# A two-layer transformer on one core: a third add on GpSimd, four rows summed by TensorE, and a softmax moved to the next pass

## The reference

```python
# 1: attention of 16 heads of 8 channels, bias -slope[h] * |i - j|
probs = softmax(q @ k.T / sqrt(8) + bias);  x = ln(x + (probs @ v) @ W_out.T + b_out)
# 2: 8 experts (top 2) and a shared one; c is the gate's weight of an expert
y = sum_e c[:, e] * ((silu(x @ W1[e] + B1) * (x @ W3[e] + B3)) @ W2[e] + B2);  x = ln(x + y + z)
# 3: a token looks back at 44 fixed offsets, of which 16 different ones are below 256
scores = stack([(q * shift(k, off)).sum(-1) * scale for off in OFFSETS], -1) + pos_bias
attn = softmax(scores)
out = sum_i attn[..., i] * shift(v, OFFSETS[i])
x = ln(x + (out * sigmoid(x @ w_gate + b_gate)) @ w_out + b_out)
# 4: 8 linear experts, top 2
x = ln(x + sum_e w[:, e] * (x @ expert_w[e].T))
```

## Time and profile before

| | |
|---|---|
| median of 3 runs | 1566.03 us |
| the profiled execution | 1564.01 us |
| its span, first to last instruction | 1562.2 us |
| mean granted clock of TensorE in it | 0.975 |
| instructions | 35071 |

### The profile page before, as it was taken

The page is one execution under the profiler, slowest core; times in us unless marked ns, Lnnn a source line. Parts: engine busy times, 40 slices in busy tenths (PEclk is TensorE's granted clock), DMA queues, the critical chain, the costliest instruction groups (busy, mean ns, idle before and its releaser), DMA issues.

```text
span 1562.2 us, 35071 instructions
## 1 busy us (share of the span) xinstructions
PE 1472.7 (94%) x12384; PEld 1171.0 (75%) x12384; DVE 1239.5 (79%) x3646; ACT 933.9 (60%) x1868; POOL 685.3 (44%) x644
## 2 busy tenths in 40 slices
PE   4899999999999999999999999999999999998855
PEld 2677788778778787788788778878887788776633
DVE  4567788888888888888888888888888888776656
ACT  1666756666666566666766666666566676654411
POOL 0024455554434455543445554334455543455531
PEclk9999999999999999999999999999999999999867
DMA  4324443344444334444443344344334434433321
GB/s 145 127 86 136 134 128 108 113 134 109 113 136 126 125 101 129 140 103 115 129 135 106 112 139 122 99 136 126 119 107 130 139 100 116 126 92 82 83 51 46
DMA packets 83563, 179.75 MB, mean 115 GB/s; under 512 B 9771, under 2 KB 65835, under 8 KB 66219
## 3 DMA queue, kind: packets, MB, share of 16 engines
q1 hardware_dynamic: 83390, 177.52, 39.9%
HBM read 151.80 MB, written 25.43 MB: 113 GB/s over the span
## 4 chain that ended last, share of the span: by engine, by line
PE 82%; DVE 8%; DMA 3%; issue 3%; POOL 2%; SPq 1%; ACT 1%; DVEq 0%; POOLq 0%; ACTq 0%
PE bTU L572 8%; PE bPV L543 8%; PE bPV L521 8%; PE bTU L573 8%; PE bS L560 7%; PE bTU L490 7%; PE bTU L463 6%; PE bTU L505 6%; PE b L581 4%; PE bS L563 3%; PE bTU L507 3%; PE b L454 2%; DVE mneg L1027 2%; PE b L437 1%; POOL prod L1098 1%
## 5 line engine op out<-in xcount | busy, mean ns | idle before, releaser
L1027 DVE TENSOR_REDUCE mneg<-bS 128x2 bf16<-128x512 f32 x512 | 339.6, 687 | 64.9 <-PE bS L563 63.4
L1090 POOL TENSOR_TENSOR prod<-prod 128x1024 f32<-128x1024 f32 x64 | 150.6, 2353 | 473.1 <-DVE prod L939 473.1
L1098 POOL TENSOR_TENSOR prod<-kC,qC 128x512 f32<-128x512 f32 x256 | 307.8, 1243 | 13.6 <-issue 13.6
L721 ACT ACTIVATE P<-bTU 128x512 f32<-128x512 f32 x512 | 287.7, 596 | 31.3 <-PE bTU L507 24.8
L1110 POOL TENSOR_TENSOR h<-ub,gBcb 128x256 f32<-128x256 f32 x256 | 183.8, 730 | 276.0 <-DVE ub L1040 264.7
L560 PE MATMUL bS<-stack 96*128 96x256 bf16 x1024 | 225.5, 279 | 15.9 <-DVE mneg L1027 7.8
L731 ACT ACTIVATE sil<-bTU,b 128x256 f32<-128x256 f32 x288 | 136.6, 475 | 155.5 <-PE bTU L573 148.3
L505 PE MATMUL bTU<-stack 97*128 97x256 bf16 x1024 | 215.2, 275 | 1.4 <-DMA stack<-mT 0.5
L563 PE MATMUL bS<-dist,identh 128*128 128x128 f16 x1024 | 200.1, 222 | 0.0
L507 PE MATMUL bTU<-dist,identh 128*128 128x128 f16 x1024 | 193.5, 220 | 0.0
L572 PE MATMUL bTU<-x1T,w 128*128 128x256 f32 x576 | 178.7, 392 | 1.1 <-DVE ub L1040 1.0
(11 more groups left out here) (156 smaller groups left out, 2634.0 us busy)
## 6 DMA issues: line engine op xcount, KB each, us to landing
prod<-d_w SPq DMA_DIRECT2D x64, 1024.0 KB, 9.5
stack<-d_parts SPq DMA_DIRECT2D x192, 192.0 KB
gBcb<-d_cB SPq DMA_DIRECT2D x32, 1024.0 KB, 5.5
d_parts<-parts SPq DMA_DIRECT2D x96, 128.0 KB, 2.0
d_w<-wT SPq DMA_DIRECT2D x32, 256.0 KB, 2.1
xT<-in_xT SPq DMA_DIRECT2D x32, 128.0 KB, 2.3
x<-in_x SPq DMA_DIRECT2D x32, 128.0 KB, 2.2
out_x<-xout SPq DMA_DIRECT2D x32, 128.0 KB, 1.9
```

The costliest lines, as they stand in the source:

```text
L721: act_f(P[k % 8][:].rearrange("p a b -> p (a b)"), bTU[turn_bank("ST", k)][:], ACT.Exp, scale=SLOPES[head(k)]).then_inc(actA2.done("exp", ...
L1027: v.tensor_reduce(mneg[:, :, k], bS[k % 2][:].rearrange("p (a b) -> p a b", a=TT), op=ALU.max, axis=AX.X, negate=True).then_inc(dveS.done( ...
L1098: tt_(prod[e % 2][:, 2 * p:2 * p + 2, :], shifted(kC, p), qC[:].unsqueeze(1).to_broadcast([128, 2, T]), ALU.mult).then_inc(poolC1.done("pr ...
```

## The change

Four things change. C2.sm sums four rows instead of eight, since GpSimd now makes a third add (C2.add.2: rows 8 to 11 onto rows 0 to 3, once the first two are done). The softmax of block 3 (steps scT, mx, exp, sum, wT, dw, wb, now named Cs) runs one pass later, in the pass of C2. Because C1.vg still runs in the pass before, the values `vC`, the gate `tg` and the residual `x2b` get two buffers each, and the scores `scs` no longer share one with `wT`. And all five orders are new.

```diff
-LAG = {..., "B2": 4, "C1": 4, "C2": 5, "C2n": 6,
+LAG = {..., "B2": 4, "C1": 4, "Cs": 5, "C2": 5, "C2n": 6,
     "pe": """
-        A1.qk S.s.0 S.s.1 B2.z A2.ST.0 S.s.2 S.s.3 A2.ST.1 A1.v A2.ST.2 A2.ST.3 S.s.4 A2.ST.4 S.s.5 A2.ST.5 A2.ST.6
+        B2.z A1.qk A1.v A2.ST.0 A2.ST.1 S.s.0 Cs.scT A2.ST.2 S.s.1 A2.ST.3 A2.ST.4 S.s.2 A2.PV.0 B.xT A2.ST.5
...
     "act": """
-        A1.qk  A2.exp.0 A2.exp.1 A2.exp.2 A2.exp.3 A2.exp.4 A2.exp.5 A2.exp.6 A3n.nm C2n.nm A2.exp.7 B.xT
+        A1.qk A2.exp.0 A2.exp.1 A2.exp.2 A2.exp.3 A3n.nm C2n.nm B2.nm Cs.exp B.xT A2.exp.4 D.xT C1.xT A2.exp.5
...
     "pool": """
-        C2.add.0 C2.add.1 C1.prod.0 C1.prod.1 C1.prod.2 C1.prod.3 C1.prod.4 C1.prod.5 C1.prod.6 C1.prod.7 A3.xbo
-        C2.xb B.h.1 B.h.2 B.h.3 B.h.4 B.h.5 B.h.6 B.h.7 B.h.8""",
+        C1.prod.0 C1.prod.1 C1.prod.2 C1.prod.3 C1.prod.4 C1.prod.5 C1.prod.6 C2.add.0 C1.prod.7 B.h.1 B.h.2 B.h.3
+        B.h.4 C2.add.1 B.h.5 C2.add.2 A3.xbo C2.xb B.h.6 B.h.7 B.h.8""",
...
-        for p in range(2):
-            pe.wait_ge(poolC2.sem, poolC2.count(e, "add", p))
-            for x in range(4):
-                i = mm(o[:, 0:T], ident[:], pv[e % 2][:, 8 * p + x, :], start=(p == 0 and x == 0),
-                       stop=(p == 1 and x == 3))
+        pe.wait_ge(poolSum.sem, poolSum.count(e, "add", 2))
+        for x in range(4):
+            i = mm(o[:, 0:T], ident[:], pv[e % 2][:, x, :], start=(x == 0), stop=(x == 3))
...
-        pool.wait_ge(dveC2.sem, dveC2.count(e, "pv", 4 * n + 3))
-        tt_(pv[e % 2][:, 8 * n:8 * n + 4, :], pv[e % 2][:, 8 * n:8 * n + 4, :], pv[e % 2][:, 8 * n + 4:8 * n + 8, :],
-            ALU.add).then_inc(poolC2.done("add", n), 1)
+        if n < 2:
+            pool.wait_ge(dveC2.sem, dveC2.count(e, "pv", 4 * n + 3))
+        else:
+            pool.wait_ge(poolSum.sem, poolSum.count(e, "add", n - 1))
+        to, frm, rows_ = ((0, 4, 4), (8, 12, 4), (0, 8, 4))[n]
+        tt_(pv[e % 2][:, to:to + rows_, :], pv[e % 2][:, to:to + rows_, :], pv[e % 2][:, frm:frm + rows_, :],
+            ALU.add).then_inc(poolSum.done("add", n), 1)
```

More of the change, by code:

```diff
@@ L61 @@
+        B.ab.8 C1.sc M.mT""",
     "dve": """
[L62 to L66, removed]
+        B2.res D2.mom N.root.0 A1.rest A1.v N.root.1 S.max.0 N.root.2 N.root.3 Cs.mx S.max.1 S.max.2 Cs.sum S.max.3
@@ L70 @@
+        B.h.4 C2.add.1 B.h.5 C2.add.2 A3.xbo C2.xb B.h.6 B.h.7 B.h.8""",
     "sp": """
-        C2.wb A1.part.0 D2.out A1.part.1 A1.part.2 X.xT B.cT A3.x A1.rows.0 B.cb A1.rows.1 A1.rows.2 C1.dw M.m C1.wb""",
+        Cs.dw A1.part.0 A1.part.1 Cs.wb B.cT C2.wb B.cb X.xT A1.part.2 A1.rows.0 A3.x A1.rows.1 A1.rows.2 D2.out M.m""",
 }
@@ L141, in network @@
         xT = sb("xT", [128, T])
[L142 removed]
+        x0, x2b = sb("x0", [128, TT, D]), [sb(f"x2b{i}", [128, TT, D]) for i in range(2)]
         x0b = x0
@@ L584, in one @@
                         i.then_inc(peC1.done("sc"), 1)
-                    if what == "C1.scT" and (e := r["C1"]) is not None:
-                        take(7, ("C1", dveC1, "sub", 0), t)
+                    if what == "Cs.scT" and (e := r["Cs"]) is not None:
+                        take(7, ("Cs", dveCs, "sub", 0), t)
                         for tt in range(TT):
@@ L615, in one @@
                             i.then_inc(peA3.done("out"), 1)
-                    if what == "C1.wT" and (e := r["C1"]) is not None:
-                        take(7, ("C1", actC1, "wT", 0), t)
-                        pe.wait_ge(dveC1.sem, dveC1.count(e, "w"))
+                    if what == "Cs.wT" and (e := r["Cs"]) is not None:
+                        take(7, ("Cs", actCs, "wT", 0), t)
+                        pe.wait_ge(dveCs.sem, dveCs.count(e, "w"))
                         wv = wn[:].rearrange("p t h a -> p t (h a)")
@@ L1053, in one @@
                         v.tensor_tensor(ds[:, :, :, 0:NS], sc_.rearrange("p t a h -> p t h a"),
                                         mC2[:].unsqueeze(3).to_broadcast([128, TT, H, NS]),
-                                        ALU.subtract).then_inc(dveC1.done("sub"), 1)
-                        v.tensor_tensor(ds[:, :, :, NS], ob, mC2[:], ALU.subtract).then_inc(dveC1.done("subo"), 1)
-                    if what == "C1.sum" and (e := r["C1"]) is not None:
-                        dve.wait_ge(actC1.sem, actC1.count(e, "exp"))
+                                        ALU.subtract).then_inc(dveCs.done("sub"), 1)
@@ L1059, in one @@
+                        v.tensor_tensor(ds[:, :, :, NS], ob, mC2[:], ALU.subtract).then_inc(dveCs.done("subo"), 1)
+                    if what == "Cs.sum" and (e := r["Cs"]) is not None:
+                        dve.wait_ge(actCs.sem, actCs.count(e, "exp"))
                         v.tensor_reduce(sC[:], es[:], op=ALU.add,
-                                        axis=AX.X).then_inc(dveC1.done("sum"), 1)
-                        dve.wait_ge(dveC1.sem, dveC1.count(e, "sum"))
-                        v.reciprocal(rC[:], sC[:]).then_inc(dveC1.done("rec"), 1)
```

124 lines of the change are left out of this document (66 added, 58 removed).

## The result

The changed kernel takes 1627.29 us (median of 4 runs, 1624.33 to 1630.68), the kernel before 1566.11 beside it: ratio 1.039, 95% interval 1.037 to 1.041. The forecast was 1606, its range 1566 to 1642. The sign and the period of a full pass were right; the passes at the end, where the program runs empty, were not.

What follows compares the result with a forecast made beforehand. TensorE's matmuls were taken to bound a full pass. 26 passes at +1.4 us (+36) and +4 outside brought 1564.0 to 1604 profiled, 1606 us as median; range 1566 to 1642 (8 in 10).

Steps and rivals of the forecast that it cites:

- TensorE as the pace, and the worth of four matmuls: A full pass lasts as long as TensorE's matmuls; four fewer in C2.sm save 1.73 us a pass.
- ScalarE at the start of a pass, +2.1: From A1.qk to A2.ST.7 ScalarE's chain takes 10.1 us, TensorE's work 8.0; TensorE waits 2.1 us a pass.
- The end of a pass, +0.5: C2.out waits for C2.gt (0.47) and, side by side, M.mT's copy in its bank (0.52): +0.5 us a pass.
- VectorE against GpSimd, +0.5: A1.lo, held beside GpSimd's products, delays D.acc for A2.ST.12 to A2.ST.14: +0.5 us a pass, bounds 0 and 1.3.
- rival 3: VectorE and GpSimd set the pace: A1.lo, gc, C2.pv held by products, C2.add.2 late; 1650 us, chance 0.15.
- The sum of a full pass, +1.4: -1.73 + 2.1 + 0.5 + 0.5 = +1.4 us a full pass, period 46.5 us, 26 passes, +36 us.
- The passes outside: Passes 2 to 5 +1 us each, 32 and 33 -2.4, 34 to 36 +2 each: together +4 us.

Runs made afterwards that it cites:

- e4: Changed kernel without the third add on GpSimd; C2.sm sums eight rows by eight matmuls at its new place: 1671.8 us, period 48.33 us.
- e1: Changed kernel with Cs.scT moved on TensorE from before A2.ST.2 to after A2.ST.3: 1625.3 us.
- e3: Changed kernel with Cs.scT after A2.ST.3 and Tanh for SiLU in the experts (no table loads inside a pass): 1619.7 us.
- e5: Changed kernel with A1.lo moved on VectorE right behind G.rank, before GpSimd's products start: 1616.4 us.
- e7: Kernel before plus third add and four-row C2.sm, softmax lag of before, similar orders; third add behind products and two B.h, C2.sm behind Cs.scT: 1631.2 us.
- e8: Kernel before plus third add and four-row C2.sm, old softmax lag; adds ahead of products, C2.sm later, G.weigh ahead of the last C2.pv: 1608.5 us.
- e10: e8 with C1.sc waiting for the products one by one instead of the last, and some steps moved, among them B.ab.5 and S.max.8: 1559.9 us.
- e11: e10 with GpSimd's eight products ahead of the adds from pass 32 on: 1598.8 us.
- e9: e8 with G.weigh behind the last C2.pv again, so that gc starts beside the second add: 1638.2 us.
- e2: Changed kernel with Tanh for SiLU in block 2's experts, leaving ScalarE no table loads inside a pass: 1626.8 us.

## Why the prediction was right, and where it wasn't

**TensorE as the pace, and the worth of four matmuls.** Right: e4 measured 1.72 for 1.73.

**ScalarE at the start of a pass, +2.1.** The chain was right (9.84 us to the end of A2.exp.4, forecast 10.1 to TensorE's step behind it), and so nearly was the size: TensorE stands 1.75 us there (1.45 at Cs.scT, 0.3 at D.xT). The place was not. Of the waits that the prediction named as its sign, A2.ST behind ScalarE's exponential and A2.PV behind ScalarE aren't there. TensorE stands at Cs.scT behind `Vz`, since Cs.scT uses the bank of A1.v, which the prediction had not followed. With that wait gone ScalarE takes 1.6 us (e1), with both gone VectorE's roots stand next (e3). The term named one of three barriers of nearly the same length; the sum came out because each of them alone is about as long, which was luck.

**The end of a pass, +0.5.** Right: 0.45 at C2.out, and by the side that the working gave as the longer, M.mT's copy. The third add made C2.sm wait for nothing in full passes.

**VectorE against GpSimd, +0.5.** Right: 0.5 us a pass at two A2.ST behind D.acc, and 0.43 came back in e5, which shortened `gc` as well. A1.lo lost 0.98, less than the 1.2 of the upper bound. By the rule of the Trainium skill (SBUF — State Buffer, Who interferes with whom) each of C2.pv.4 to C2.pv.7 would be held too where it meets a GpSimd instruction that reads SBUF and began first. The trace agrees for A1.lo and `gc`. Of the 128 C2.pv.4 to C2.pv.7, 56 took over 0.75 us (up to 2.01), all of them beside GpSimd, and 45 met nothing there; the median of all C2.pv stayed at 0.685, their mean rose to 0.811 from 0.683. Behind them TensorE waits only at A3.aT, 0.2 us a pass, for A3.num, which stands behind C2.pv.7. So rival 3 was there in part, and in full passes its cost is at most that.

**The sum of a full pass, +1.4.** Measured +1.51.

**The passes outside.** This is where the prediction failed. In its sum the passes until pass 7 had 4 x 1 + 1.4 = +5.4, and 6.7 came. The end from pass 31 on had 1.4 - 2.4 + 2 = +1, and 23.5 came. The change cost 66.5 us where the sum had 40. Of the 26.5 between them 22.5 lie at the end, 2.6 in the period and 1.3 at the start. The step was: "The softmax moves from pass 35's end to pass 36's start, so its latency at the end of the kernel is the same". But pass 35 holds block 3's way of sequence 30 as well, and doesn't get shorter when the softmax of sequence 31 leaves it. The changed kernel's C2.sm and Cs.scT of the last passes (TensorE):

```profile
1558.57 3.64 PE L581 MATMUL b<-prod,hsum 128*32 128x256 f32 x32 [8.71 <-POOL prod L1102]
1565.17 3.75 PE L463 MATMUL bTU<-prod,ident 128*128 128x256 f32 x8 [2.96 <-POOL prod L1094]
1569.53 1.19 PE L469 MATMUL b<-woc,gat 128*128 128x128 f32 x4 [0.60 <-DVE gat L1008]
1571.24 1.12 PE L589 MATMUL b<-ident,scs 128*128 128x128 f32 x4 [0.52 <-DVE nCy L1014]
1602.77 3.75 PE L463 MATMUL bTU<-prod,ident 128*128 128x256 f32 x8 [16.68 <-POOL prod L1094]
```

and the kernel before:

```profile
1505.16 3.64 PE L581 MATMUL b<-prod,hsum 128*32 128x256 f32 x32 [5.25 <-POOL prod L1098]
1515.37 1.08 PE L622 MATMUL b<-ident,wn 128*128 128x128 f32 x4 [4.50 <-DVE wn L1065]
1531.18 3.75 PE L463 MATMUL bTU<-prod,ident 128*128 128x256 f32 x8 [1.88 <-POOL prod L1090]
1536.71 1.99 PE L463 MATMUL bTU<-prod,ident 128*128 128x256 f32 x8 [1.77 <-POOL prod L1090]
```

Before, the last sequence went from C1.sc to the end of C2.sm in 1538.70 - 1505.16 = 33.5 us, and now in 1606.52 - 1558.57 = 48.0: Cs.scT stands behind C2.sm and C2.out of the sequence before it (12.7 us after C1.sc's start; before 4.6), and the sum waits for a third add. That is 14.4 of the 23.5 us; 10.4 are there already when C1.sc of pass 35 starts (211.7 us after A1.qk of pass 31, before 201.3), and behind the last C2.sm it is 1.3 less. From C2.out of pass 35 to that of pass 36 it takes 37.6 us. The granted clock fell too (0.82 in the mean from A1.qk of pass 31 on, before 0.87; 0.85 in e4), with more waits of TensorE there; by rows a C2.sm of four matmuls takes 3.75 at that clock and 1.89 in full passes.

Is it the third add or the lag? e4 has the lag and the orders and no third add, and ends 283.8 us after A1.qk of pass 31, 25.4 more than before. So the lag with its orders is enough for the whole of the end; how the two divide was not measured. The lag isn't the only way to it: e7 and e8 have the old lag and the cut, and end 279.2 and 277.2 us after A1.qk of pass 31, where before needs 258.3; e10, whose C1.sc doesn't wait for the last product, needs 266.3.

In the last passes of e7, e8 and e10 the loop softmax, weights, C2.pv, adds, products, softmax seems to be the pace, as it was before the change at about 40.5 us: e11 has the adds behind products of 10.1 us, and its passes there are 10.3 and 7.9 us longer than those of e10. That each microsecond put into the loop costs one is not shown beyond that.

The 6.7 us until pass 7 were not tested, but the rows place 5.1 of them: from A1.qk to A1.qk pass 5 takes 44.95 us (before 41.76) and pass 6, where only D2 is missing, 46.64 (before 44.69). In pass 5 the granted clock stood at 0.5 for 3.4 us.

That the time lay inside the range is luck in part. The range's upper end, 1642, was worked out for VectorE and GpSimd as the pace of the full passes (rival 3), which they weren't, and no bound was put on the end of the kernel.

## What to carry to other kernels

A wait at a step says which barrier came last, and how many stand right behind it only an experiment tells: before paying for the removal of one, sum the readiness of everything that the next few steps need. And where waits change, look at the granted clock of each pass before putting a longer period down to them (e9). Where the engine that sets the pace gets less work, look at the full-length chain beside it, and at the granularity of its waits: here eight waits in place of one for the eighth product, together with small moves around them, took 1608.5 to 1559.9, 48.6 us, and the four matmuls themselves were worth 44.5 (e4). And the passes in which a pipeline fills and drains have their own pace, the loop through one sequence; sum them apart, with what every sequence has in each pass.

## What was not expected of the hardware

- The hold between VectorE and GpSimd is as long for the smallest instruction as for a large one: `gc` with 32 columns, 0.19 us alone (e8), stood for 1.90 us beside an add of 2.36 (e9), and 1.08 beside a product; A1.lo with 512 columns lost 0.98. What is queued behind it waits as well: in e9 TensorE waits longer for the maxima (1.6 us a pass) than for `gc` itself (0.7).
- In e9 the waits by themselves cost nothing net, and the clock did: behind 0.62 and 1.45 us of waiting, 1.7 us apart, the granted clock stood at 0.5 for 3.4 us in 20 of 24 passes, and each of these is 1.6 us longer than the other four.
- The third table load of a pass was worth nothing (e2), since ScalarE was not alone in being late. The two that the change itself takes away (ScalarE is busy 861.5 us against 933.9) were not tested apart.
